# A two-layer routed transformer block: load semaphores, branch order and who compares, changed in three places

## The chip, the cores and the metric

The kernel runs on one core of one Trainium2 chip. The metric is the device time of one execution in microseconds (us); the time given for a kernel is the median over its runs. TensorE, VectorE, ScalarE, GpSimd and SyncE (which here only issues DMAs) are named PE, DVE, ACT, POOL and SP in the rows of the profile, PEld is the weight-load side of TensorE.

## The reference, cut to what matters

The input is x of 16 sequences by 256 tokens by 256. Layer 0 is causal attention (16 heads of 64, one key/value head, an added bias, a null key, and a mask of the keys), a layer norm, and then a top-1 router with a capacity; layer 1 is two further mixture layers, which the change does not touch.

```python
logits = tokens @ router_w.T                      # 4096 tokens, 8 experts
top1_idx = jnp.argmax(probs, axis=-1)
top1_prob = jnp.max(probs, axis=-1)
order = jnp.lexsort((-top1_prob, top1_idx))       # by expert, then by falling probability
...
keep_sorted = pos_in_group < capacity             # 640 places for each expert
return jnp.where(keep, top1_idx, 0)               # who finds no place goes to expert 0
```

So each token needs its place among the tokens of its expert: how many have a larger probability, or the same and a smaller number.

## The kernel before, in words

**Two cases.** The mask marks keys that may be seen, and in the data given only the last 64 positions of each sequence have any. The first DVE instructions reduce the mask to one number (`early_i`); every engine reads it (`early_keys`, L578) and branches. In the late case, the one that runs, attention, routing and the first experts are computed only for the last 64 positions of the 16 sequences, 1024 tokens, and one null row that stands for all others. In the general case all 4096 tokens are computed; that code is in the program but is not run.

**How TensorE's code lies.** Each engine's program is a straight list with branches. TensorE's (from L1322) has `If(late)` with attention and ranking (`late_rank`), then the `Else` with the whole general case, then a second `If(late)` with `late_table` and the experts. After ranking, TensorE therefore branches over the general code.

**The start.** SP issues the mask, two chunks of x (`x_l`), then g_in and wkv on the semaphore `ld_q` (L655, L656), reads `early_i`, and issues wq on the same semaphore (L659). Whoever waits for g_in or wkv waits for `ld_q` at 48, that is for wq too: TensorE before the key/value projection (`project_late_kv`, L1117 and L1121), ACT before it scales the turned rows by g_in (`late_rows`, L1691), DVE before it copies the key weights (L2164). The query projection `project_late_q` (L1128) needs wq. Then come the scores (`late_scores`, L1136), DVE's biased scores (L2103, L2106, L2107), ACT's exponential (L1712), DVE's probabilities (L2112 to L2115), the transposes (`turn_late`, L1143), the weighted sum (`weigh_late`, L1150) and the output projection (`project_late_o`, L1156).

**Attention's loop.** There are 8 chunks of 128 rows, `attend_late(c)` on each engine. On TensorE, chunk c computes scores, projects keys and queries of chunk c+1, waits for `v_ev` at c+2 (values of c+1, written by DVE's `late_values`, L2084), projects the output of chunk c-1, waits for the probabilities and turns them. DVE computes, in chunk 0 only, statistics of the other six chunks of x (`rest_stats`, L2143 and L2147) before `late_values(1)`. GpSimd adds the mask to the bias (`masked_bias`, L892), which DVE's L2103 waits for.

**The ranking.** The 1024 keys (probabilities) lie one per partition in `key_l`, 8 columns, and once more as one row repeated in all partitions: PE turns them into banks 0 and 1, ACT copies them to `rows_s` in SBUF (L1788, on `l_rows_ev`). For each column m of 128 tokens the matrix `beats[m]` (128 by 1024, bf16) holds whether key m is larger than the row's (for tokens up to this block, "is_lt", width (m+1)·128, L2417 on DVE or L907 on GpSimd) or not smaller ("is_le" for the later blocks, width (7-m)·128, L2423; for m = 0 in two pieces, L2419 and L2421), and `tied[m]` (L2424) settles equal keys inside the block. DVE does all of it but the "is_lt" of m = 5, 6, 7, which GpSimd does (`NGB = 3`). TensorE sums `beats[m]` against the one-hot choices, 9 small matmuls for each m (L1248, L1249), in the order m = 0 to 7:

```python
for m in range(NTW):
    pe.wait_ge(l_beat, m + 1)
    if m >= NTW - NGB:
        pe.wait_ge(l_beat_g, m - NTW + NGB + 1)
```

DVE takes the sums up at L2434 and goes through some 50 small dependent instructions; TensorE builds the row table (`late_table`, L1258), DVE writes it (L2487, semaphore `table`), GpSimd gathers the first expert's rows (`gathers`, L910; it waits for `table` just before its branch), TensorE turns them (L1273) and multiplies by the first weights (`expert_up`, L1285).

**Memory and loads.** The weights w1 (8 MB) are loaded from 16.8 us on (L712), w2 (8 MB) from 121.8 us on (L723).

## Time and profile before

| | |
|---|---|
| median of 3 runs | 596.69 us (596.47 to 598.17) |
| the profiled execution's own time | 598.48 us |
| its span, first to last instruction | 596.7 us |
| mean granted TensorE clock | 0.968 |
| TensorE busy | 539.6 us (90%) |
| VectorE busy | 319.9 us (54%) |
| ScalarE busy | 237.2 us (40%) |
| GpSimd busy | 235.7 us (39%) |

The page gives the busy time of each engine and the chain of waits that ended last, followed back from the last instruction. A busy share is a mean over stages; which engine sets the pace is read from a stage's timeline, where each group has its start, its duration, and in brackets how long its engine had been idle and what ended that.

### The profile page before, as it was taken

The numbers are of one execution on the slowest core, as the hardware profiler recorded it, in microseconds if no ns is written. First come the engines' busy times: TensorE is split into PE (matmuls) and PEld (weight loads), VectorE is DVE, ScalarE is ACT, GpSimd is POOL, SyncE is SP. The second block draws the span as 40 slices with busy tenths as digits, with TensorE's granted clock in tenths as the row PEclk, the third lists the DMA queues.
The fourth block names the chain that finished last, engine by engine and source line by source line (L and its number), as shares of the span: only waits on it lengthen the run. The fifth ranks groups of instructions, "written<-read, shape, count | busy, mean of one in ns | idle before, by whom it ended". The sixth has DMA issues, their size and how long they took to land.

```text
span 596.7 us, 11286 instructions
## 1 busy us (share of the span) xinstructions
PE 539.6 (90%) x3716; PEld 458.0 (77%) x3716; DVE 319.9 (54%) x968; ACT 237.2 (40%) x663; POOL 235.7 (39%) x319
## 2 busy tenths in 40 slices
PE   2899998941899999999999999999999998998885
PEld 2788886721799999998878978888888786776664
DVE  2767758577122224752537954444444354666564
ACT  1465445520111111115544245555555454443432
POOL 1412211041211121004825465555555078777860
PEclk9999999875799999999999999999999999999998
DMA  6980000185996531522378025665555324655552
GB/s 127 345 345 2 1 2 1 63 361 215 279 311 229 181 113 47 152 89 63 89 238 268 1 64 154 161 161 160 158 158 150 93 72 124 186 172 173 168 168 74
DMA packets 53205, 88.28 MB, mean 148 GB/s; under 512 B 11250, under 2 KB 43891, under 8 KB 51604
## 3 DMA queue, kind: packets, MB, share of 16 engines
q1 hardware_dynamic: 45028, 65.29, 31.7%
q0 software_dynamic: 8112, 22.16, 15.4%
q8 instruction: 36, 0.59, 0.4%
q14 instruction: 29, 0.24, 0.1%
HBM read 62.38 MB, written 25.04 MB: 146 GB/s over the span
## 4 chain that ended last, share of the span: by engine, by line
PE 71%; POOL 13%; issue 6%; DVE 5%; DMA 3%; ACT 2%; SPq 1%; DVEq 0%; POOLq 0%; ACTq 0%
POOL arena L910 11%; PE psum L1285 10%; PE psum L1524 10%; PE psum L1296 9%; PE psum L1443 7%; PE psum L1156 6%; PE psum L1538 5%; PE psum L1128 5%; PE psum L1453 3%; PE psum L1516 3%; POOL iota_i L939 2%; PE psum L1136 2%; PE psum L1471 1%; PE psum L1532 1%; PE psum L1150 1%
## 5 line engine op out<-in xcount | busy, mean ns | idle before, releaser
L910 POOL DMA_INDIRECT arena<-x,row_tok x71 | 68.3, 962 | 53.5 <-PE psum L1516 44.4
L910 POOL DMA_INDIRECT arena<-y_sorted,pos_k_i x64 | 65.3, 1021 | 35.8 <-DMA y_sorted<-arena 15.6
L1524 PE MATMUL psum<-big_w,arena 128*128 x284 | 72.9, 379 | 0.0
L1820 ACT ACTIVATE arena<-psum,arena 128x128 f32<-128x128 f32 x64 | 18.3, 368 | 118.2 <-PE psum L1285 88.0
L1285 PEld LDWEIGHTS psum<-arena,big_w 128*128 128x128 f32 x512 | 61.6, 197 | 2.8 <-issue 1.2
L1285 PE MATMUL psum<-arena,big_w 128*128 128x128 f32 x512 | 62.0, 281 | 1.5 <-DVE arena L2506 1.5
L1590 PE MATMUL psum<-big_w,arena 128*128 x256 | 63.3, 380 | 0.0
L1443 PE MATMUL psum<-arena,big_w 128*128 128x256 f32 x256 | 59.9, 381 | 0.2 <-ACT arena L1839 0.2
L1524 PEld LDWEIGHTS psum<-big_w,arena 128*128 128x128 f32 x284 | 53.7, 190 | 7.2
L1296 PE MATMUL psum<-arena 128*128 128x256 f32 (+1 forms) x256 | 57.7, 379 | 0.0
L2742 DVE SCALAR_TENSOR_TENSOR arena<-arena 128x128 f32<-128x128 f32 x71 | 20.8, 293 | 60.8 <-ACT arena L1906 60.4
L1443 PEld LDWEIGHTS psum<-arena,big_w 128*128 128x128 f32 x256 | 47.2, 190 | 7.1 <-ACT arena L1839 0.9
L1296 PEld LDWEIGHTS psum<-arena 128*128 128x128 f32 x256 | 47.5, 190 | 5.8
L1590 PEld LDWEIGHTS psum<-big_w,arena 128*128 128x128 f32 x256 | 46.4, 189 | 6.3 <-issue 0.5
L910 POOL DMA_INDIRECT arena<-h_late,row_tok x16 | 15.4, 963 | 86.1 <-PE psum L1273 72.8
L1538 PE MATMUL psum<-big_w,arena 128*128 x142 | 44.1, 392 | 0.7 <-ACT arena L1903 0.7
L892 POOL TENSOR_TENSOR arena<-arena 128x512 f32<-128x512 f32 x16 | 19.1, 1195 | 57.7 <-DVE arena L2107 57.6
L1156 PE MATMUL psum<-arena 128*128 128x256 f32 x144 | 34.5, 395 | 2.4 <-ACT arena L1707 1.6
L1903 ACT COPY arena<-psum 128x256 f32<-128x256 f32 x71 | 26.5, 373 | 22.6 <-PE psum L1538 22.2
L1156 PEld LDWEIGHTS psum<-arena 128*128 128x128 f32 x144 | 27.8, 198 | 7.4 <-issue 2.4
L1128 PE MATMUL psum<-arena 128*128 128x128 f32 x256 | 31.9, 285 | 0.0
L1453 PE MATMUL psum<-big_w,arena 128*128 128x256 f32 x128 | 30.6, 382 | 1.3 <-ACT arena L1843 1.3
(322 smaller groups left out, 961.3 us busy)
## 6 DMA issues: line engine op xcount, KB each, us to landing
y_sorted<-arena SPq DMA_DIRECT2D x71, 128.0 KB
big_w<-w SPq DMA_DIRECT2D x8, 1024.0 KB, 4.7
tokens<-x SPq DMA_DIRECT2D x4, 1024.0 KB, 14.9
x<-tokens SPq DMA_DIRECT2D x16, 256.0 KB, 2.8
z_kept<-arena SPq DMA_DIRECT2D x16, 256.0 KB
out<-arena SPq DMA_DIRECT2D x16, 256.0 KB
y_late<-arena SPq DMA_DIRECT2D x16, 128.0 KB, 1.7
big_w<-expert_w_t SPq DMA_DIRECT2D x1, 2048.0 KB, 7.5
```

The costliest lines, as they stand in the source:

```text
L910: pool.indirect_dma_start(dst, None, rows, bass.IndirectOffsetOnAxis(ap=idx, axis=0)).then_inc(done, 16)
L1128: mm = pe.matmul(bank[a][:, (j % 4) * P:(j % 4 + 1) * P], wq_s[:, k, j * P:(j + 1) * P], xt_l[:, k, :], start=k == 0, stop=k == KD - 1)
L1156: mm = pe.matmul(bank[6][:, 0:D], lhs(j), wo_s[:, j, :], start=j == 0, stop=j == NPAIR - 1)
L1285: mm = pe.matmul(bank[1 + 2 * u + f // 4][:, (f % 4) * P:(f % 4 + 1) * P], big_w[:, c:c + P], g_t[:, k, :], start=k == 0, stop=k == KD - 1)
L1296: mm = pe.matmul(bank[5 + j % 2][:, 0:D], act_t[j % 2][:, f, :], arena[:, bass.ds(e * (NF * D) + f * D, D)], start=f == 0, stop=f == NF - 1)
L1443: mm = pe.matmul(bank[up_bank(b) + q][:, half * S:(half + 1) * S], w[:, k, q * M1:(q + 1) * M1], p_s[:, unit(b)[1][k], :], start=k == 0, s ...
L1453: mm = pe.matmul(bank[6][:, n * D:(n + 1) * D], mid[u][q][:, n * P:(n + 1) * P], md_s[:, E1 + q, :], start=q == 0, stop=q == NSH - 1)
L1524: mm = pe.matmul(bank[2 + i % RT][:, 0:2 * M1], c_gt[i % RT][:, k, :], mgu_s[:, k, bass.ds(e, 1), :].rearrange("p a m -> p (a m)"), start= ...
L1538: pe.matmul(bank[5][:, 0:D], c_midt[i % RT], md_s[:, bass.ds(e, 1), :].rearrange("p a d -> p (a d)"), start=True, stop=True).then_inc(c_dn, 1)
L1590: mm = pe.matmul(o, z_t[u][:, k, n * P:(n + 1) * P], ew_s[:, k, bass.ds(e, 1), :].rearrange("p a d -> p (a d)"), start=False, stop=n == NB ...
L1903: act.copy(c_y[t % RT], bank[5][:, 0:D]).then_inc(c_yc, 1)
L2742: dve.scalar_tensor_tensor(c_mid[v], c_leak[v], 0.01, c_leak[v], ALU.mult, ALU.max).then_inc(c_lkd, 1)
```

## The change

It has four parts. (1) g_in and wkv get a semaphore of their own (`ld_kv`, the same one as `ld_wo`), and key/value work waits for these two alone; wq keeps `ld_q`, waited for at 16. (2) DVE computes `late_values(1)` before `rest_stats` in chunk 0. (3) TensorE's general code comes first in the program, the late case last and in one piece, so that the branch over the general code is taken at the start; and GpSimd waits for `table` after its branch. (4) The comparisons are shared out anew: GpSimd takes the "is_le" of m = 1 and the "is_lt" of 5 and 3; ACT takes the "is_lt" of 7, 6 and 4, each as Relu(key - row) followed by Sign; TensorE sums in the order 0, 1, 2, 5, 7, 3, 6, 4.

```diff
-        NGB = 3
+        G_LT, A_LT, G_LE = (5, 3), (7, 6, 4), 1
+        over = [tokens[:, NC - 6 - 2 * u:NC - 4 - 2 * u, :].rearrange("p c d -> p (c d)").bitcast(BF16) for u in range(2)]
...
+        ld_kv = ld_wo
+        l_beat_a, l_beat_a0 = xsd, 2
+        l_over, l_over0 = x_ev, NTW
...
             for dst, src in ((gin[:, :], g_in), (wkv_r, wkv.rearrange("(k p) n -> p k n", p=P))):
-                sp.dma_start(dst, src).then_inc(ld_q, 16)
+                sp.dma_start(dst, src).then_inc(ld_kv, 16)
...
+                sp.wait_ge(ld_kv, 32)
                 sp.dma_start(wo_s, wo.rearrange("(j p) n -> p j n", p=P)).then_inc(ld_wo, 16)
...
                 pool.wait_ge(l_rows_ev, 2)
-                for m in range(NTW - NGB, NTW):
+                pool.tensor_scalar(beats[G_LE][:, (G_LE + 1) * P:], rows_s[:, (G_LE + 1) * P:], key_l[:, G_LE:G_LE + 1], None, ALU.is_le).then_inc(l_beat_g, 1)
+                for m in G_LT:
                     pool.tensor_scalar(beats[m][:, 0:(m + 1) * P], rows_s[:, 0:(m + 1) * P], key_l[:, m:m + 1], None, ALU.is_lt).then_inc(l_beat_g, 1)
...
-            pool.wait_ge(table, 1)
             with pool.If(general):
...
             with pool.Else():
                 pool.wait_ge(l_hs, 48)
+                pool.wait_ge(table, 1)
                 gathers(TILES_L, h_late, True)
...
-                    pe.wait_ge(ld_wo, 16)
+                    pe.wait_ge(ld_wo, 48)
...
-                for m in range(NTW):
+                order = (0, 1, 2, 5, 7, 3, 6, 4)
+                for n, m in enumerate(order):
                     pe.wait_ge(l_beat, m + 1)
-                    if m >= NTW - NGB:
-                        pe.wait_ge(l_beat_g, m - NTW + NGB + 1)
+                    if m == G_LE:
+                        pe.wait_ge(l_beat_g, 1)
+                    if m in G_LT:
+                        pe.wait_ge(l_beat_g, G_LT.index(m) + 2)
+                    if m in A_LT:
+                        pe.wait_ge(l_beat_a, l_beat_a0 + A_LT.index(m) + 1)
...
             pe.wait_ge(const, NCONST)
-            late = early_keys(pe) == 0
-            with pe.If(late):
+            general = branch(pe)
+            with pe.If(general):
+                pe.sem_inc(turned, NPN)
...
+                experts(TILES, False)
+            with pe.Else():
                 turn_late_x(0)
-                pe.wait_ge(ld_q, 48)
+                pe.wait_ge(ld_kv, 32)
                 pe.wait_ge(setup, 1)
                 project_late_kv(0)
+                pe.wait_ge(ld_q, 16)
                 project_late_q(0)
...
                 late_rank()
-            with pe.Else():
-                pe.sem_inc(turned, NPN)
...
-                experts(TILES, False)
-            with pe.If(late):
                 late_table()
                 experts(TILES_L, True)
...
-                act.wait_ge(ld_q, 48)
+                act.wait_ge(ld_kv, 32)
                 late_rows(0)
...
+                act.wait_ge(l_rows_ev, 2)
+                for n, m in enumerate(A_LT):
+                    w = (m + 1) * P
+                    if n >= 2:
+                        act.wait_ge(l_beat_a, l_beat_a0 + n - 1)
+                    act.activation(over[n % 2][:, 0:w], rows_s[:, 0:w], ACT.Relu, bias=key_l[:, m:m + 1], scale=-1.0).then_inc(l_over, 1)
+                    act.wait_ge(l_over, l_over0 + n + 1)
+                    act.activation(beats[m][:, 0:w], over[n % 2][:, 0:w], ACT.Sign).then_inc(l_beat_a, 1)
...
+                if not last:
+                    late_values(c + 1)
                 if c == 0:
                     rest_stats()
-                if not last:
-                    late_values(c + 1)
...
-                dve.wait_ge(ld_q, 48)
+                dve.wait_ge(ld_kv, 32)
...
-                    if m < NTW - NGB:
+                    if m not in G_LT and m not in A_LT:
                         dve.tensor_scalar(beats[m][:, 0:(m + 1) * P], rows[:, 0:(m + 1) * P], key, None, ALU.is_lt)
...
-                    elif m < NTW - 1:
+                    elif m < NTW - 1 and m != G_LE:
                         dve.tensor_scalar(beats[m][:, later], rows[:, later], key, None, ALU.is_le)
```

How the instructions stand, at the places where it matters (in these listings branches are shown, waits are not, and equal neighbours are one row).

VectorE in the ranking, before, from the comparisons of m = 1 on (TENSOR_SCALAR is a comparison, SCALAR_TENSOR_TENSOR the settling of equal keys):

```order
L2417 TENSOR_SCALAR arena<-psum,arena 128x256
L2423 TENSOR_SCALAR arena<-psum,arena 128x768
L2424 SCALAR_TENSOR_TENSOR arena<-psum,arena,before 128x128
L2417 TENSOR_SCALAR arena<-psum,arena 128x384
L2423 TENSOR_SCALAR arena<-psum,arena 128x640
L2424 SCALAR_TENSOR_TENSOR arena<-psum,arena,before 128x128
L2417 TENSOR_SCALAR arena<-psum,arena 128x512
L2423 TENSOR_SCALAR arena<-psum,arena 128x512
L2424 SCALAR_TENSOR_TENSOR arena<-psum,arena,before 128x128
L2417 TENSOR_SCALAR arena<-psum,arena 128x640
L2423 TENSOR_SCALAR arena<-psum,arena 128x384
```

And in the changed kernel, the same stretch:

```order
L2439 TENSOR_SCALAR arena<-psum,arena 128x256
L2446 SCALAR_TENSOR_TENSOR arena<-psum,arena,before 128x128
L2439 TENSOR_SCALAR arena<-psum,arena 128x384
L2445 TENSOR_SCALAR arena<-psum,arena 128x640
L2446 SCALAR_TENSOR_TENSOR arena<-psum,arena,before 128x128
L2445 TENSOR_SCALAR arena<-psum,arena 128x512
L2446 SCALAR_TENSOR_TENSOR arena<-psum,arena,before 128x128
L2445 TENSOR_SCALAR arena<-psum,arena 128x384
```

Three comparisons are gone: 768 wide (m = 1), 512 wide (m = 3) and 640 wide (m = 4).

TensorE at the row table, before: the end of the general case (L1296 is an expert's second product) and then the second `If(late)`, where the late case arrives by a branch from behind L1253:

```order
L1296 MATMUL psum<-arena 128x256
L1370 UNCONDITIONAL_BRANCH
L1405 COMPARE_AND_BRANCH
L1258 MATMUL psum<-arena 128x16 x8
L1273 MATMUL psum<-ident,arena 128x128 x2
L1285 MATMUL psum<-arena,big_w 128x128 x16
```

In the changed kernel the same instructions follow the ranking directly:

```order
L1261 MATMUL psum<-arena 128x8 x8
L1262 MATMUL psum<-arena 128x8
L1266 MATMUL psum<-arena,ones 128x8
L1271 MATMUL psum<-arena 128x16 x8
L1286 MATMUL psum<-ident,arena 128x128 x2
L1298 MATMUL psum<-arena,big_w 128x128 x16
```

ScalarE behind its copies of the keys' row (L1801), in the changed kernel; the six activations are new, and no table load stands between them:

```order
L1796 ACT_TABLE_LOAD
L1796 ACTIVATE act_warm<-eps_col 128x1
L1798 ACTIVATE arena<-arena 128x72
L1801 COPY tokens<-psum 128x512 x2
L1807 ACTIVATE tokens<-tokens,arena 128x1024
L1809 ACTIVATE arena<-tokens 128x1024
L1807 ACTIVATE tokens<-tokens,arena 128x896
L1809 ACTIVATE arena<-tokens 128x896
L1807 ACTIVATE tokens<-tokens,arena 128x640
L1809 ACTIVATE arena<-tokens 128x640
```

## Rows read from the trace of the kernel before

**Rows 1.** The page, section 4: chain of work that ended last, shares by engine.

```profile
PE 71%; POOL 13%; issue 6%; DVE 5%; DMA 3%; ACT 2%; SPq 1%; DVEq 0%; POOLq 0%; ACTq 0%
```

**Rows 2.** Timeline 0 to 20 us (start us, us, engine, line, op, xcount [idle <-releaser]).

```profile
7.07 0.69 PE L1111 MATMUL psum<-ident,arena 128*128 128x128 f32 x2 [7.07 <-DVE arena L2080]
...
10.54 0.63 ACT L1691 ACTIVATE arena<-psum,gin 128x128 f32<-128x128 f32 x2 [4.18 <-DMA arena<-wq]
...
13.04 5.29 PE L1128 MATMUL psum<-arena 128*128 128x128 f32 x32
...
16.21 0.37 DVE L2170 COPY arena<-nb_bc 64x8 f32<-64x8 f32 x2 [5.16 <-DMA nb_bc<-null_bias]
...
17.73 2.36 POOL L892 TENSOR_TENSOR arena<-arena 128x512 f32<-128x512 f32 x2
...
19.78 0.70 DVE L2103 TENSOR_TENSOR arena<-psum,arena 128x520 f32<-128x520 f32 x1 [1.75 <-PE psum L1136]
```

**Rows 3.** DMA issues, 0 to 60 us (KB each, median us from issue to landing).

```profile
arena<-wo SPq DMA_DIRECT2D x1, 1024.0 KB, 7.2
...
arena<-wkv SPq DMA_DIRECT2D x1, 128.0 KB, 2.5
```

**Rows 4.** Timeline, end of chunk 0, 23 to 31 us.

```profile
23.94 2.05 DVE L2143 BATCH_NORM_STATS2 arena<-arena 128x6 f32<-128x256 f32 x6
...
26.70 3.72 PE L1156 MATMUL psum<-arena 128*128 128x256 f32 x16 [0.86 <-DVE arena L2084]
...
29.09 0.69 DVE L2115 TENSOR_TENSOR arena<-arena 128x512 f32<-128x512 f32 x1
...
30.26 1.04 PE L1143 MATMUL psum<-ident,arena 128*128 128x128 f32 x8
```

**Rows 5.** Timeline, the comparisons, 127 to 137 us.

```profile
127.08 7.54 POOL L907 TENSOR_SCALAR arena<-tokens,arena 128x768 bf16<-128x768 f32 x3 [32.02 <-ACT tokens L1788]
...
135.59 0.60 DVE L2424 SCALAR_TENSOR_TENSOR arena<-psum,arena,before 128x128 bf16<-128x128 f32 x2
...
136.25 0.37 PE L1248 MATMUL psum<-arena 128*128 128x8 bf16 x8
...
136.75 0.22 DVE L2434 TENSOR_TENSOR arena<-psum,arena 128x64 f32<-128x64 f32 x1 [0.18 <-PE psum L1249]
```

**Rows 6.** Groups by line and shape, 125 to 137 us (busy us, mean ns).

```profile
L907 POOL TENSOR_SCALAR arena<-tokens,arena 128x768 bf16<-128x768 f32 x1 | 2.2, 2217 | 32.0 <-ACT tokens L1788 32.0
...
L2423 DVE TENSOR_SCALAR arena<-psum,arena 128x768 bf16<-128x768 f32 x1 | 1.0, 1009 | 0.0
...
L2423 DVE TENSOR_SCALAR arena<-psum,arena 128x512 bf16<-128x512 f32 x1 | 0.7, 743 | 0.0
```

**Rows 7.** Groups by line and shape, ScalarE, 0 to 160 us.

```profile
L1774 ACT CAST arena<-iota_f 128x1024 f16<-128x1024 f32 x1 | 1.1, 1083 | 0.0
```

**Rows 8.** Chain of waits, 143 to 147 us (start us, us, what).

```profile
144.37 0.99 issue
```

**Rows 9.** Timeline, row table to first expert, 146 to 158.5 us.

```profile
146.07 0.17 DVE L2487 CAST row_tok<-psum 128x16 int32<-128x16 f32 x1 [0.37 <-PE psum L1258]
...
147.31 1.19 POOL L910 DMA_INDIRECT arena<-h_late,row_tok  x1 [12.70 <-issue]
...
151.82 5.86 PE L1285 MATMUL psum<-arena,big_w 128*128 128x128 f32 x32 [0.79 <-DVE arena L2506]
...
157.51 0.38 PE L1273 MATMUL psum<-ident,arena 128*128 128x128 f32 x2
...
158.17 0.95 POOL L910 DMA_INDIRECT arena<-h_late,row_tok  x1 [5.92 <-PE psum L1273]
```

**Rows 10.** DMA queues, 138 to 139 and 142 to 143 us (packets, MB, share).

```profile
q8 instruction: 1, 0.02, 5.5%
...
q8 instruction: 1, 0.02, 5.8%
```

**Rows 11.** Timeline, last output projections, 104 to 111 us.

```profile
104.77 5.38 PE L1156 MATMUL psum<-arena 128*128 128x256 f32 x16 [1.59 <-ACT arena L1707]
```

More of the change, by code:

```diff
@@ L931, in _ @@
                 pool.wait_ge(l_hs, 48)
+                pool.wait_ge(table, 1)
                 gathers(TILES_L, h_late, True)
@@ L1241, in late_rank @@
                 mm.then_inc(l_out, 1)
-                for m in range(NTW):
+                order = (0, 1, 2, 5, 7, 3, 6, 4)
+                for n, m in enumerate(order):
                     pe.wait_ge(l_beat, m + 1)
-                    if m >= NTW - NGB:
-                        pe.wait_ge(l_beat_g, m - NTW + NGB + 1)
+                    if m == G_LE:
[4 more added lines that the diff above has]
+                        pe.wait_ge(l_beat_a, l_beat_a0 + A_LT.index(m) + 1)
                     for c in range(NTW):
-                        pe.matmul(bank[4][:, c * E0:(c + 1) * E0], beats[m][:, c * P:(c + 1) * P], oh_l[:, m, :], start=m + c == 0, stop=False)
-                    mm = pe.matmul(bank[4][:, m * E0:(m + 1) * E0], tied[m], oh_l[:, m, :], start=False, stop=m == NTW - 1)
+                        pe.matmul(bank[4][:, c * E0:(c + 1) * E0], beats[m][:, c * P:(c + 1) * P], oh_l[:, m, :], start=n + c == 0, stop=False)
+                    mm = pe.matmul(bank[4][:, m * E0:(m + 1) * E0], tied[m], oh_l[:, m, :], start=False, stop=n == NTW - 1)
                 mm.then_inc(l_won, 1)
```

64 lines of the change are left out of this document (33 added, 31 removed).

## The prediction

> **What bounds the kernel now.** I read the page's chain first: 71% of the span is TensorE's, 13% GpSimd's [rows 1]. It names the engines, not the places, so I went on to the timeline of the stages that the change touches, all before 160 us. There TensorE is not the pace. At the start it waits for the first rows (7.07 us), then ACT, which scales them, waits till 10.54 for the load of wq, which it does not use, and the query projection starts at 13.04 [rows 2]. In chunk 0 the output projection waits until 26.70 for a small DVE instruction (L2084) that stands behind the statistics, which begin at 23.94 [rows 4]. In the ranking DVE is the pace and TensorE follows it [rows 5]. Behind it come two gaps: 0.99 us with no work at all before the row table [rows 8], and 1.07 us from the table's end (146.07 + 0.17) to GpSimd's gather at 147.31 [rows 9]. From chunk 1 on TensorE runs without gaps, so a shift at the end of chunk 0 is handed down to all that follows.
>
> **The sum, part by part.** Less than 1.8 us (0.3%) is about what a measurement can't tell from no change.
>
> Start. wkv lands 2.5 us after its issue, before 7 us [rows 3], so ACT may begin when the transposes end, 7.07 + 0.69 = 7.76, not at 10.54: 2.8 us earlier. Scaling and the key/value projection together lie between 10.54 and 13.04, 2.5 us, and would end near 10.3; the query projection then waits for wq, which landed at 10.5, and starts at 10.55 instead of 13.04, a gain of 2.5. Not all of it counts. DVE's first biased scores (L2103, at 19.78) also need the masked bias, which GpSimd starts at 17.73, two instructions in 2.36, so the first is ready at 17.73 + 1.18 = 18.91; its inputs hang on the load that ends at 16.21 [rows 2], which does not move. What is late next is thus the mask, and the gain there is 19.78 - 18.95 = **0.83**. The changed wait for wo costs nothing: wo lands 7.2 us after its issue at 16.3, at 23.5 to 24 [rows 3], and is needed at 25 or later.
>
> Chunk 0. DVE's L2084 goes ahead of the statistics, 2.05 us and their sums [rows 4]. The output projection loses its 0.86 of waiting beyond the shift of 0.83 and ends at 28.7 instead of 26.70 + 3.72 = 30.4. The transposes behind it (30.26) need DVE's last probabilities, which ended at 29.09 + 0.69 = 29.78 [rows 4] and move by 0.83 to 28.95: they start at 29.0. So DVE becomes the bound, and the two edits together give 30.26 - 29.0 = **1.25** (0.83 if the reorder gives nothing).
>
> Comparisons. DVE loses three: 768, 512 and 640 wide. The first two took 1.009 and 0.743 [rows 6], the third lies midway at 0.876; neighbours overlap by 0.08 each, so 2.63 - 0.25 = 2.38 us. DVE's last one ended at 135.59 + 0.60 = 136.19, now 133.81. TensorE had one group of nine matmuls left, 0.4 us (136.25 to 136.65) [rows 5]; now the groups of 7, 3, 6 and 4 are left, and behind each other each takes 0.26 more: 133.86 + 0.41 + 3 x 0.26 = 135.05. DVE goes on at 135.1 instead of 136.75: **1.6**. The cover must hold: GpSimd's three take at most 3 x 2.217 = 6.65 from 127.08 [rows 5, 6], 133.7, and its last is wanted at 134.3; ACT's six, at most 1.083 each (the 1024-wide cast [rows 7]), end by 133.5 plus the gaps between them (0 to 0.2 each), 134.5 at worst, and the last is wanted at 134.8. If that cover goes, TensorE waits for them one for one.
>
> Order of the cases. TensorE no longer branches between ranking and row table. The 0.99 us that nothing explains [rows 8] stand just behind that branch; in them no engine works, and instruction blocks came in at 138 and 142 us [rows 10]. I take the branch for the cause: **0.99**, bounds 0 and 0.99. GpSimd's branch goes ahead of its wait: 1.07 shrinks to the delay of a gather that waits for TensorE without a branch, 158.17 - (157.51 + 0.38) = 0.28 [rows 9]: **0.8**, bounds 0 and 0.8. In exchange TensorE takes the long branch at about 5 us. It costs nothing as long as the first transposes, at 7.07 now, start by about 9.0, for from there the way through both projections just meets the mask at 18.95; later than that, it costs one for one. The nearest price is the row table: from the branch at 138.1 at the latest to 145.36, at most 7.2 us; the bounds are 0 and 12.1 - 9.0 = 3.1. I take 0.
>
> The Trainium skill (Runtime: NRT & Kernel Launch, Instruction fetch mechanics) speaks against that exchange: a taken branch to code that is not at hand holds execution until a block is fetched. Here no row shows a branch of TensorE at 5 us; by that rule there is a fetch on both sides of the exchange, and it is one of the rivals below.
>
> Sum: 1.25 + 1.6 + 0.99 + 0.8 = **4.65 us**. The profiled execution took 598.48, 1.79 above the median. One row accounts for that: sixteen matmuls of the output projection took 5.38 at a granted clock of half, against 3.72 in chunk 0 [rows 4, 11], 1.66 more. So the profiled run would give 593.8 with that fall of the clock, and the median without it 596.69 - 4.65 = **592.0**. How the clock falls is not mine to shift, but the first expert's 32 matmuls run at half clock for their first 4.3 us (5.86 [rows 9]), and that stretch may come out 2 us cheaper or dearer by where the new times fall: plus or minus 1.7 for the range.
>
> **The rivals.**
> (a) The branch at the start is paid for: the first transposes come at up to 12.1, the start costs up to 3.1 instead of 0, and the time is 595.1. For it: the 7.2 us at the row table. Against: those lay in a stretch with 8 MB of w2 in flight, while at 5 us only wkv and 1 MB of wq are.
> (b) The 0.99 us are not the branch's (a wake-up of TensorE, or code that is late in any order): 593.0. For it: the second block came at 142, long after the branch.
> (c) ACT or GpSimd become the bound of the ranking: ACT's dependent pairs are new here. With gaps of 0.5 between them ACT ends 1.2 us behind what TensorE wants: 593.2.
> (d) Slower: TensorE's code up to 25 us lies ready now; after a branch at 5 us every further block must be brought in, and from 16.8 to 44 us 8 MB of w1 are in flight. If a block is as late as the gap between the two at 138 and 142 us [rows 10], 4.7 us, one such block eats the whole gain and two give 592.0 + 9.4 = 601.4. It decides from 6.5 us of lost fetch time (4.65 + 1.8). Against: TensorE had a block during 16 to 44 us before too, with no gap behind it.
>
> **How the numbers follow.** Forecast 0.56, (a) 0.18, (b) 0.12, (c) 0.09, (d) 0.05. All but (d) and the far end of (a) are faster; faster by over 0.3% means below 594.9. Faster: 0.56 + 0.12 + 0.09, and half of (a) that ends below 594.9, with 0.02 off for the clock: 0.84. Same: the rest of (a), and the clock's share, 0.12. Slower: 0.04. The range goes from 592.0 - 1.7 = 590.3 to (a) at 595.0.
>
> **What would show it.** Right: the first projection of keys at 8.5 and DVE's first biased scores at 18.9, waiting for GpSimd; the transposes of chunk 0 at 29.0; DVE through with the comparisons 7.1 us after its first (9.5 now) and TensorE's last sums within 1.3 us of that; less than 0.2 us between DVE's one-hots and the row table; about 0.3 us from table to gather. Wrong: a TensorE start after 9 us (a), a gap of 1 us still before the row table (b), TensorE waiting for ACT or GpSimd in the sums (c), gaps of TensorE that end with no releaser between 5 and 44 us (d). If chunk 1 starts no earlier than 30.2, my reading of the start is wrong.

## The result, and the profile after

The change is faster. Over 17 runs each the median went from 596.45 to 593.58 us; the ratio is **0.9939, 95% interval 0.9926 to 0.9952**, or 3.6 us (2.9 to 4.4); the two medians by themselves are 2.9 us apart. One of the change's 17 runs took 1924.93 us and, as the only slow one, is left out of the ratio. The forecast was 592.0, range 590.3 to 595.0. The profiled execution took 594.12 us (span 592.3) against 598.48 (span 596.7).

Lines have moved: L1111 is now L1119, L1128 is L1136, L1143 is L1151, L1156 is L1164, L2103 is L2125, L2434 is L2456, L2487 is L2509, L910 is L917, L1285 is L1298.

The page's chain of the changed kernel hardly differs from [rows 1]: TensorE 68% for 71, GpSimd 14% for 13, VectorE 6% for 5.

```profile
PE 68%; POOL 14%; DVE 6%; issue 6%; SPq 2%; DMA 2%; ACT 1%; DVEq 0%; POOLq 0%; ACTq 0%
```

The timeline of the start, 0 to 20 us (start, us, engine, line, operation, operands [idle before <- what ended it]), to be read beside [rows 2]:

```profile
8.54 0.69 PE L1119 MATMUL psum<-ident,arena 128*128 128x128 f32 x2 [8.54 <-issue]
9.32 0.63 ACT L1704 ACTIVATE arena<-psum,gin 128x128 f32<-128x128 f32 x2 [2.83 <-PE psum L1119]
...
11.83 5.55 PE L1136 MATMUL psum<-arena 128*128 128x128 f32 x32
...
16.72 0.37 DVE L2192 COPY arena<-nb_bc 64x8 f32<-64x8 f32 x2 [9.16 <-DMA nb_bc<-null_bias]
...
18.26 2.37 POOL L898 TENSOR_TENSOR arena<-arena 128x512 f32<-128x512 f32 x2 [0.70 <-DVE arena L2197]
...
19.58 0.70 DVE L2125 TENSOR_TENSOR arena<-psum,arena 128x520 f32<-128x520 f32 x1 [1.01 <-POOL arena L898]
```

ACT now waits for TensorE and not for wq, and the query projection begins 1.2 us earlier. But TensorE's first transposes are 1.5 us later and end a wait on nothing shown ("issue"). The first biased scores, now held by GpSimd's mask, gained 0.20 us, because the null bias and with it the mask are 0.5 later than before.

The end of chunk 0, to be read beside [rows 4]: the output projection comes 1.2 us earlier, the transposes behind it 0.62 (29.64 against 30.26).

```profile
25.48 3.66 PE L1164 MATMUL psum<-arena 128*128 128x256 f32 x16
...
28.89 0.69 DVE L2137 TENSOR_TENSOR arena<-arena 128x512 f32<-128x512 f32 x1
...
29.64 1.09 PE L1151 MATMUL psum<-ident,arena 128*128 128x128 f32 x8 [0.50 <-DVE arena L2137]
```

The comparisons, 124 to 137 us, beside [rows 5]:

```profile
126.57 1.15 ACT L1807 ACTIVATE tokens<-tokens,arena 128x1024 bf16<-128x1024 f32 x1
126.63 2.21 POOL L912 TENSOR_SCALAR arena<-tokens,arena 128x768 bf16<-128x768 f32 x1 [32.14 <-ACT tokens L1801]
...
128.83 3.75 POOL L914 TENSOR_SCALAR arena<-tokens,arena 128x768 bf16<-128x768 f32 x2
...
131.47 0.74 ACT L1809 ACTIVATE arena<-tokens 128x640 bf16<-128x640 bf16 x1
...
132.66 0.60 DVE L2446 SCALAR_TENSOR_TENSOR arena<-psum,arena,before 128x128 bf16<-128x128 f32 x2
...
134.27 0.17 PE L1262 MATMUL psum<-arena 128*128 128x8 bf16 x1
...
134.55 0.22 DVE L2456 TENSOR_TENSOR arena<-psum,arena 128x64 f32<-128x64 f32 x1 [0.91 <-PE psum L1262]
```

ScalarE is done at 132.21 and GpSimd at 132.58, both before VectorE's last tie ends at 133.26, and TensorE's last sum ends at 134.44 (134.27 + 0.17). Only once does TensorE wait for a helper, 0.62 us for GpSimd's m = 1 at 128.99; the next group waits for VectorE again, so this costs nothing. From the first comparison (126.12, before 126.67) to the take-up of the ranks it is 8.43 us, before 10.08.

From the one-hots to the experts, beside [rows 8, 9]:

```profile
141.46 0.68 DVE L2497 TENSOR_TENSOR arena<-arena 128x1024 f16<-128x1024 f16 x1
...
142.20 0.69 PE L1271 MATMUL psum<-arena 128*128 128x16 f16 x8 [5.76 <-DVE arena L2497]
...
143.14 0.35 DVE L2507 CAST pos_i<-arena 64x8 int32<-64x8 f32 x2
143.50 0.17 DVE L2509 CAST row_tok<-psum 128x16 int32<-128x16 f32 x1
...
144.56 1.19 POOL L917 DMA_INDIRECT arena<-h_late,row_tok  x1 [11.98 <-issue]
...
148.97 5.28 PE L1298 MATMUL psum<-arena,big_w 128*128 128x128 f32 x32 [0.79 <-DVE arena L2528]
...
155.16 3.84 PE L1298 MATMUL psum<-arena,big_w 128*128 128x128 f32 x32 [0.70 <-DVE arena L2528]
```

The gap ahead of TensorE's row table is gone: 142.20 starts 0.06 us behind the one-hots, before it was 1.01. But the row numbers, which GpSimd waits for, show no idle time before them any more: VectorE works through its small operations without a pause until 143.50. From the start of the one-hots to the row numbers it is 2.04 us, before 2.40. The first expert starts 2.85 us earlier than in [rows 9], the second 3.44 (155.16 against 158.60), because the 32 matmuls between them took 5.28 us, before 5.86. From there every stage up to 350 us is 3.44 us earlier. What comes on top later in the profiled pair (4.21 us at the last output) arises in layer 2, where nothing was changed.

### The profile page after: what moved, and what is told of

Read it like the earlier page. It is cut to its first block, busy times and chain, and to the rows that moved or that the text cites. A ratio compares the mean times of both kernels' runs of the same rounds, so it can differ in the third digit from the quotient of the medians.

```text
span 592.3 us, 11290 instructions
## 1 busy us (share of the span) xinstructions
PE 537.5 (91%) x3716; PEld 457.6 (77%) x3716; DVE 318.3 (54%) x965; ACT 242.6 (41%) x669; POOL 233.3 (39%) x319
## 4 chain that ended last, share of the span: by engine, by line
PE 68%; POOL 14%; DVE 6%; issue 6%; SPq 2%; DMA 2%; ACT 1%; DVEq 0%; POOLq 0%; ACTq 0%
POOL arena L917 11%; PE psum L1298 10%; PE psum L1537 10%; PE psum L1309 9%; PE psum L1456 7%; PE psum L1551 5%; PE psum L1164 5%; PE psum L1136 4%; PE psum L1466 3%; PE psum L1529 3%; POOL iota_i L947 3%; PE psum L1144 1%; PE psum L1484 1%; PE psum L1545 1%; PE psum L1158 1%
## 5 line engine op out<-in xcount | busy, mean ns | idle before, releaser
L917 POOL DMA_INDIRECT arena<-x,row_tok x71 | 68.2, 960 | 51.9 <-PE psum L1529 43.4
L917 POOL DMA_INDIRECT arena<-y_sorted,pos_k_i x64 | 65.7, 1027 | 36.4 <-POOL iota_i L947 18.9
L1298 PEld LDWEIGHTS psum<-arena,big_w 128*128 128x128 f32 x512 | 61.0, 196 | 2.8 <-issue 1.2
L1298 PE MATMUL psum<-arena,big_w 128*128 128x128 f32 x512 | 61.4, 279 | 1.5 <-DVE arena L2528 1.5
L917 POOL DMA_INDIRECT arena<-h_late,row_tok x16 | 15.4, 960 | 84.7 <-PE psum L1286 72.1
L1164 PE MATMUL psum<-arena 128*128 128x256 f32 x144 | 34.5, 394 | 1.6 <-ACT arena L1720 1.6
L1136 PE MATMUL psum<-arena 128*128 128x128 f32 x256 | 32.1, 286 | 0.8 <-DVE arena L2129 0.8
L1164 PEld LDWEIGHTS psum<-arena 128*128 128x128 f32 x144 | 27.8, 198 | 6.4 <-issue 2.4
L2781 DVE SCALAR_TENSOR_TENSOR arena<-arena,w_k 128x256 f32<-128x256 f32 x64 | 28.2, 482 | 6.9 <-issue 5.2
```

The lines of the kernel that those rows point to most:

```text
L917: pool.indirect_dma_start(dst, None, rows, bass.IndirectOffsetOnAxis(ap=idx, axis=0)).then_inc(done, 16)
L1136: mm = pe.matmul(bank[a][:, (j % 4) * P:(j % 4 + 1) * P], wq_s[:, k, j * P:(j + 1) * P], xt_l[:, k, :], start=k == 0, stop=k == KD - 1)
L1164: mm = pe.matmul(bank[6][:, 0:D], lhs(j), wo_s[:, j, :], start=j == 0, stop=j == NPAIR - 1)
L1298: mm = pe.matmul(bank[1 + 2 * u + f // 4][:, (f % 4) * P:(f % 4 + 1) * P], big_w[:, c:c + P], g_t[:, k, :], start=k == 0, stop=k == KD - 1)
L2781: m = dve.scalar_tensor_tensor(z_s[u][:, n, :], yk[u][:, 2 * n + k, :], w_k[:, k, bass.ds(b * NB + n, 1)], base, ALU.mult, ALU.add)
```

## The experiments

For the runs the four parts of the change are taken as three, named here K (the key/value semaphore and the swap of values and statistics in chunk 0), O (TensorE's general case first in its program, so that the late case runs from the ranking into the row table without a branch, and GpSimd's branch ahead of its wait) and S (the shared comparisons). With the kernel before and the change itself, six runs complete the eight combinations. Each ratio is to the kernel before as it ran in the same job. The two edits inside K, and the two inside O, were not timed apart.

**K alone**, edit against the kernel before:

```diff
-                sp.dma_start(dst, src).then_inc(ld_q, 16)
+                sp.dma_start(dst, src).then_inc(ld_kv, 16)
-                act.wait_ge(ld_q, 48)
+                act.wait_ge(ld_kv, 32)
-                if c == 0:
-                    rest_stats()
                 if not last:
                     late_values(c + 1)
+                if c == 0:
+                    rest_stats()
```

> The kernel before with only the load semaphore of its own and the earlier values of chunk 1 (parts 1 and 2). Theory (the mask is what DVE's first biased scores wait for, and the block fetches of TensorE's branch at 5 us had held up the loads that the mask hangs on by 0.5 us): without that branch the first transposes are back at 7.1, the copy of the null bias on DVE at 16.2, the first biased scores at 18.95 and chunk 0's transposes at 29.0, 1.25 earlier than before; time 1.2 us below before. Rival (the 0.5 us are chance, nothing to do with the fetches): the copy of the null bias lies anywhere between 16.2 and 16.8, as in kernels with the branch. Rival (the start is worth only what the change showed, 0.6, because of the queue itself): first biased scores at 19.6 here too.

Measured 0.9991 (0.9974 to 1.0007). The forecast was 1.2 us, this is 0.5, and it can't be told from no change. In its profile the start gained more than the forecast gave it: mask 17.28, first biased scores 18.60 (before 19.78), turn of chunk 0 at 28.66 (before 30.26). Of that 0.39 us can't be put down to the edit: SyncE's issue of the null value, behind which the null bias is issued, took 2.79 us in this execution and 3.18 both before and in K and S. The branch gap stayed, 1.18 us.

**O alone**:

```diff
-            late = early_keys(pe) == 0
-            with pe.If(late):
+            general = branch(pe)
+            with pe.If(general):
...
-            with pe.If(late):
                 late_table()
                 experts(TILES_L, True)
```

> The kernel before with only part 3 (TensorE's rare case first in the program, GpSimd waiting for the table after its branch). Theory (the branch behind the ranking held TensorE 1 us, but DVE's own five small instructions ahead of the table take the place of that wait): the gap between DVE's one-hots and TensorE's row table falls from 0.99 to under 0.1, the table comes 0.35 us earlier, counted from the one-hots, and the gather 0.2 nearer to the table; time 0.5 us below before, less than its noise. TensorE's first transposes at 8.5 instead of 7.1, the null bias copied at 16.7; that costs nothing, since the key work waits for wq anyway. Rival (the gap belongs to TensorE's wake-up): the gap stays at 1 us. It did not in the change, so this rival would need parts 1 or 4 for it.

Measured 1.0026 (1.0009 to 1.0043): by itself this part costs 1.5 us, where 0.5 us of gain were expected. The start of its timeline:

```profile
8.05 0.69 PE L1112 MATMUL psum<-ident,arena 128*128 128x128 f32 x2 [8.05 <-DVE arena L2080]
10.68 0.62 ACT L1691 ACTIVATE arena<-psum,gin 128x128 f32<-128x128 f32 x2 [4.27 <-DMA arena<-wq]
...
11.45 1.19 PE L1118 MATMUL psum<-arena 128*128 128x128 f32 x4 [2.71 <-ACT arena L1691]
...
13.18 6.12 PE L1129 MATMUL psum<-arena 128*128 128x128 f32 x32
...
20.75 0.70 DVE L2103 TENSOR_TENSOR arena<-psum,arena 128x520 f32<-128x520 f32 x1 [2.34 <-PE psum L1137]
```

The query projection takes 6.12 us, before 5.29 [rows 2], because the clock rose at 18.0 and not at 16.2; the first biased scores are 1.0 us late. The gap at the row table is 0.07, but it returns only part of that. The profiled execution took 595.54 us, 2.0 less than this kernel's median, so its rows show where time can go and not that the 1.5 us went there.

**S alone**:

```diff
-        NGB = 3
+        G_LT, A_LT, G_LE = (5, 3), (7, 6, 4), 1
...
-                    if m < NTW - NGB:
+                    if m not in G_LT and m not in A_LT:
+                    act.activation(over[n % 2][:, 0:w], rows_s[:, 0:w], ACT.Relu, bias=key_l[:, m:m + 1], scale=-1.0).then_inc(l_over, 1)
```

> The kernel before with only part 4 (comparisons shared with ScalarE and GpSimd). Theory (DVE alone set the pace of the ranking): from DVE's first comparison to its take-up of the sums 10.08 us before, 8.4 here as in the change; time 1.65 us below before, and the 0.99 us ahead of the row table are back, as the branch is. Rival (the branch needs a fixed time from its block fetch on, hidden before by the ranking): as the ranking ends earlier, TensorE is not ready earlier, the gap grows from 1.0 to up to 2.6, and the part gives nothing by itself.

Measured 0.9973 (0.9955 to 0.9992). First comparison to take-up 8.43 us, before 10.08. The gap at the row table was expected back at 0.99 us, or by the rival grown to 2.6. With the branch still there it was 0.23 us, before 1.01, so both missed:

```profile
139.84 0.68 DVE L2492 TENSOR_TENSOR arena<-arena 128x1024 f16<-128x1024 f16 x1
...
140.75 0.67 PE L1267 MATMUL psum<-arena 128*128 128x16 f16 x8 [5.93 <-DVE arena L2492]
```

**K and S (the change without O)**: the diff of O taken back from the changed kernel.

```diff
-            general = branch(pe)
-            with pe.If(general):
+            late = early_keys(pe) == 0
+            with pe.If(late):
```

> The changed kernel with part 3 taken back. Theory (parts add, each by its stage): first transposes at 7.1, null bias copied at 16.2, first biased scores at 18.95, chunk 0's transposes at 29.0, gap ahead of the row table at least 1.0 again; time within 0.3 us of the changed kernel, since the start's 0.6 comes back and the row table's and the gather's 0.5 go. Rival (fixed time from the block fetch on, as in the run with part 4 alone): the gap is 2.6, time 1 to 1.5 us above the changed kernel.

Measured 0.9948 (0.9929 to 0.9966), gap 0.26 us instead of 1.0, and one-hots to row numbers 2.04 us: the same as in the change. O can't be told from nothing here. The first biased scores came at 19.07, near the forecast; chunk 0's transposes came at 30.74 instead of 29.0, as the clock fell to the low level from 19.4 to 26.2 us.

**O and S (the change without K)**:

```diff
-                act.wait_ge(ld_kv, 32)
+                act.wait_ge(ld_q, 48)
```

> The kernel before with TensorE's rare case placed last and with the shared comparisons, but without the key/value semaphore and without the swap of chunk 0's statistics and values. The start branch alone cost 0.26% in the kernel before, the shared comparisons alone gave 0.27%, the key/value part alone 0.09%. If the parts add: ratio 0.9999. If the three help each other (the whole gave 0.61% where the singles sum to 0.10%): the key/value part covers what the start branch costs, and this run lies near 0.997, with the first biased scores after 20.3 and the turn of chunk 0 after 30.8. Ratio of 0.994 would mean that the key/value part is worth nothing.

Measured 0.9976 (0.9958 to 0.9994), with the first biased scores at 20.28 and the turn of chunk 0 at 30.76.

**K and O (the change without S)**:

```diff
-        G_LT, A_LT, G_LE = (5, 3), (7, 6, 4), 1
+        NGB = 3
```

> The kernel before with the key/value semaphore, the swap of chunk 0 and TensorE's rare case placed last, but with the comparisons split as before (three of GpSimd, none of ScalarE). It completes the table of the three parts. Theory (parts: key/value -0.24%, order +0.07%, shared comparisons -0.40%, of which 1.6 us are the comparisons and 0.7 us the wait at the row table, which the branch's late code made): here the order part removes the wait at the table (0.06 instead of 1.0 to 1.2 us, of which VectorE's small operations keep about 0.65) and the start is covered, so the ratio is about 0.9985, with the first comparison to take-up 10.1 us. Rival (the order part is worth its 1.8 us when the key/value part covers its cost at the start): 0.996. Second rival (it costs as it did alone, 0.26%): 1.0015 or more.

Measured 0.9979 (0.9965 to 0.9992), first comparison to take-up 10.09 us, gap 0.07.

The eight ratios together:

| | neither K nor S | K | S | K and S |
|---|---|---|---|---|
| without O | 1 | 0.9991 | 0.9973 | 0.9948 |
| with O | 1.0026 | 0.9979 | 0.9976 | 0.9939 |

Each part's worth is the mean of its four differences: K -0.0030 (1.8 us), S -0.0040 (2.4 us), O +0.0002 (0.1 us slower). With intervals of some 0.0017 on each ratio, such a mean is good to about 0.7 us. So K and S are each shown to gain, and O is not shown to do anything on the whole.

**The branch gap.** Four of these kernels branch between ranking and row table. The trace has each DMA packet with its time; TensorE's own instruction queue fetched a second 16 KB block there. How its end stands to the row table, in us:

| kernel | second block ends | one-hots end | row table starts | block to table |
|---|---|---|---|---|
| before | 143.75 | 144.35 | 145.36 | 1.61 |
| K | 140.73 | 141.15 | 142.33 | 1.60 |
| S | 139.15 | 140.52 | 140.75 | 1.60 |
| K and S | 140.17 | 141.52 | 141.78 | 1.61 |

That made a forecast possible. The test puts matmuls that nothing reads between the kept counts and the branch of the kernel without O:

```diff
                 pe.matmul(bank[6][:, 0:E0], ones[:, :], ksum, start=True, stop=True).then_inc(l_out, 1)
+                for _ in range(12):
+                    pe.matmul(bank[7][:, 0:P], ident[:, :], ident[:, :], start=True, stop=True)
```

> The changed kernel with TensorE's two halves as before (the branch between the ranking and the row table is back) and 12 filling matmuls of float32 between the kept counts and that branch. In the four kernels that have the branch, TensorE's row table started 1.60 to 1.62 us after the end of the second 16 KB code block that TensorE fetches there. Theory (the wait of 1.0 us at the row table is that code coming late, and its request follows TensorE's own progress): with the filling ahead of the branch the second block is requested later, at 141 or after, the row table again starts 1.6 us after its end, and the wait behind the one-hots grows from 0.26 us to 1.5 us or more. Rival (the code is fetched ahead, whatever TensorE's queue does, and the wait is a plain cost of the branch): the wait stays between 0.2 and 1.2 us, and the distance of 1.6 us from the block breaks.

```profile
139.13 0.68 DVE L2503 TENSOR_TENSOR arena<-arena 128x1024 f16<-128x1024 f16 x1
...
142.80 0.68 PE L1275 MATMUL psum<-arena 128*128 128x16 f16 x8 [3.37 <-issue]
143.52 0.17 DVE L2515 CAST row_tok<-psum 128x16 int32<-128x16 f32 x1 [2.36 <-PE psum L1275]
...
144.76 1.19 POOL L917 DMA_INDIRECT arena<-h_late,row_tok  x1 [14.48 <-issue]
```

The filling ended at 139.4, the second block came from 140.25 to 141.20, and the table started 1.60 us after it. The gap grew to 2.99 us. The block began 8.03 us after the take-up of the ranks, in K and S 5.30 us after it. So the wait is code arriving late, and work in TensorE's queue ahead of the branch puts the code off. The Trainium skill (Runtime: NRT & Kernel Launch, Instruction fetch mechanics) says that a taken branch out of the code at hand forces a fetch before execution goes on; the trace agrees, with 1.60 us from the end of the fetch as a further part of the price. What exactly sets the request stays open: the block began 0.8 us after TensorE's last matmul here, and 3.4 to 4.3 us after it in the four kernels of the table. This kernel ran once (597.54 us), so its time says nothing.

The same run also tests the forecast for the start, as it has K and S and TensorE doesn't branch at 5 us in it. The null bias was copied at 16.09, the first biased scores came at 18.95 and chunk 0's transposes at 29.00; the forecast was 18.95 and 29.0, with the null bias at 16.2.

**Null transfers first**, against the change:

```diff
-                sp.dma_start(v_null, null_kv[1:2, :].rearrange("a d -> (a d)").partition_broadcast(P)).then_inc(ld_bias, 16)
                 load_null()
+                sp.dma_start(v_null, null_kv[1:2, :].rearrange("a d -> (a d)").partition_broadcast(P)).then_inc(ld_mask, 16)
-                pool.wait_ge(ld_bias, 80)
+                pool.wait_ge(ld_bias, 64)
-                dve.wait_ge(ld_bias, 80)
+                dve.wait_ge(ld_bias, 64)
+                dve.wait_ge(ld_mask, 32)
```

> The changed kernel, but SyncE issues the null bias and null column transfers ahead of the null value, and the null value counts on a semaphore of its own, so that GpSimd's causal fill waits for the four side transfers alone. Theory (the masked bias of GpSimd bounds the first biased scores, and its input is late): the null bias copy moves from 16.7 to about 14, GpSimd's fill from 14.99 to about 13.5, its mask from 18.26 to about 16.5 at most, the first biased scores from 19.58 to 18.8 (there TensorE's first scores are next), the turn of chunk 0's probabilities from 29.64 to about 28.9, and the kernel is 0.7 us faster than the changed one: ratio to the kernel before about 0.9927. Rival (key/value and query work of TensorE, at the low clock, bound the start): first biased scores stay at 19.4 or later and the ratio stays at 0.994. A second rival: the start gains but the end does not, because a later clock fall takes it: turn at 28.9, ratio 0.994.

```profile
9.20 4.05 SPq L672 DMA_DIRECT2D null_col<-null_kv  x2
13.30 0.59 SPq L672 DMA_DIRECT2D nb_bc<-null_bias  x1
...
16.09 0.37 DVE L2192 COPY arena<-nb_bc 64x8 f32<-64x8 f32 x2 [8.50 <-DMA nb_bc<-null_bias]
...
19.03 0.70 DVE L2125 TENSOR_TENSOR arena<-psum,arena 128x520 f32<-128x520 f32 x1 [1.02 <-POOL arena L898]
...
25.86 3.69 PE L1164 MATMUL psum<-arena 128*128 128x256 f32 x16 [0.77 <-issue]
```

And of its DMA issues (KB, us from issue to landing):

```profile
arena<-wo SPq DMA_DIRECT2D x1, 1024.0 KB, 8.9
```

GpSimd's fill came at 13.19 as expected, but the null bias was issued only 0.43 us earlier (13.30, in the change 13.73): SyncE's long issue, 3.01 us for the null value there, now befell the first of the two null columns (3.40 of the row's 4.05). The scores gained 0.55 and still wait for the mask, so the mask is the bound there. The turn gained 0.25, not 0.7: TensorE was free at 25.09, but the output projection started at 25.86. The load of wo, which it needs, was issued at 16.86 and landed at 25.8. So wo was the next bound, which no run tested by an edit. In the change it was close: issued at 16.82, landed 8.5 us later at about 25.4, and wanted at 25.48. The whole, 0.9933 (0.9908 to 0.9958), is too wide to show 0.3 us.

**Row numbers first**, against the change:

```diff
+                dve.wait_ge(tab_ps, 1)
+                dve.tensor_copy(row_tok[:, 0:TILES_L], bank[3][:, 0:TILES_L]).then_inc(l_in, 1)
                 bx = [P, TILES_L, E0 - 1]
...
-                pool.wait_ge(table, 1)
+                pool.wait_ge(l_in, 4)
```

> The changed kernel, but VectorE writes the row numbers right after the one-hots, ahead of the tile numbers and the null positions, on a semaphore that only GpSimd's gather waits for. Theory (in the changed kernel VectorE's seven small operations took the place of the wait for TensorE's row table, so that only 0.4 of the 1.0 us came through): row numbers 1.5 us after the start of the last one-hots instead of 2.04, gather and expert 0 about 0.55 us earlier, ratio to the kernel before about 0.993. Rival (the gap itself, or GpSimd's own wake-up, bounds the hand-over): the row numbers come earlier but the gather does not, its distance grows from 1.06 to 1.6 us, ratio 0.994.

```profile
141.35 0.69 DVE L2497 TENSOR_TENSOR arena<-arena 128x1024 f16<-128x1024 f16 x1
...
142.82 0.17 DVE L2499 CAST row_tok<-psum 128x16 int32<-128x16 f32 x1 [0.78 <-PE psum L1271]
143.87 1.19 POOL L917 DMA_INDIRECT arena<-h_late,row_tok  x1 [11.07 <-issue]
```

The row numbers come 1.47 us after the start of the one-hots, 0.57 sooner than in the change, and the gather keeps its distance (1.05). So VectorE's small operations had taken the place of the gap. The time, 0.9934 (0.9909 to 0.9959), can't show it by itself.

**Filling at two places**, against the change: the same matmuls, 12 behind the kept counts, 10 behind the row table.

```diff
+                idle_work(12)
...
                 mm.then_inc(tab_ps, 1)
+                idle_work(10)
```

> The changed kernel with 12 float32 matmuls 128 x 128 into an unused bank behind the kept counts and 10 more behind the row table, where TensorE idles 5.8 and 4.6 us; they write nothing that is read. At the low clock they take about 0.43 us each, 5.1 and 4.3 us, so they end before TensorE is wanted. Theory (the granted clock costs time at expert 0: it comes back only at 152.0, 3 us after the first expert's matmuls begin): the clock is high at 148, the 32 matmuls of expert 0 take about 3.5 us instead of 5.3, and the second expert starts 1.5 us earlier against the first; ratio to the kernel before 0.991. Rival (something else, ScalarE and VectorE or the gathers, paces the experts): matmuls faster, the second expert no earlier, ratio 0.994. If the filling matmuls delay the table or the rows: 0.995 or more.

The clock rose at 140.5 as hoped. The second filling then took 2.5 us at the high clock, TensorE idled 2.33, and at 147.3 the clock fell again: expert 0's matmuls took 5.44 us. So this kernel did not make the state that the theory is about, and tells nothing of its worth: 5.44 lies within the 5.20 to 6.09 us of the kernels without filling. Ratio 0.9931 (0.9904 to 0.9958).

**Null first, row numbers first and that filling:**

```diff
+                dve.tensor_copy(row_tok[:, 0:TILES_L], bank[3][:, 0:TILES_L]).then_inc(l_in, 1)
...
+                idle_work(12)
...
+                idle_work(10)
```

> The changed kernel with the null transfers first, the row numbers first and the smaller filling (12 and 10 matmuls at the two idle stretches around the row table). Singly they gave 0.55 us at the first biased scores, 0.57 us at the row numbers, and a clock that rose at 140.5 but fell again at 147.3, for 0.2 to 0.4 us at expert 0. If the gains add and reach the end: 1.5 us faster than the changed kernel, ratio 0.9915. If a gain at the start is lost again to the clock's own phase: 0.993.

Measured 0.9927 (0.9907 to 0.9947), which is not to be told from the change, nor from the 0.9915 that was hoped for. In this one the clock fell at 140.7, so the second filling took 4.03 us at the low clock and left no gap behind it; the clock was high from 144.1, the 32 matmuls took 3.81 us, and in the profiles the experts ran 7.64 us earlier than in the kernel before. The filling is that of the run above; what differed was when the clock changed. In layer 2 that lead shrank to 5.9 us; a fall of the clock at 560.5, for 3.4 us, is part of it.

**The same with filling in every idle stretch** from the logits to the first rows:

```diff
+                idle_work(8)
...
+                    idle_work((5, 1, 3, 6, 1, 0, 0, 0)[n])
...
+                idle_work(18)
...
+                idle_work(18)
```

> The changed kernel with the null transfers first, the row numbers written first, and float32 matmuls of 128 x 128 into an unused bank in every idle stretch of TensorE from the logits to the first rows (8, 5, 1, 3, 6, 1, 18 and 18 of them, sized to the high clock, 0.21 us each). Theory (the clock is held up if TensorE is never idle for long, and costs time at expert 0 otherwise): the granted clock stays high from 120 to the end, expert 0's 32 matmuls take about 3.7 us, the transposes ahead of the ranking and the rows are 0.2 to 0.3 us shorter each, and the kernel is 3 us faster than the changed one: ratio to the kernel before 0.989. Rival (the clock falls all the same, and the filling, at 0.43 us each, then delays the ranks by 2 and the table by up to 2.6 us): 0.996 or more. In between, the clock up in part: 0.992.

Measured **0.9902 (0.9873 to 0.9932)**, median 591.48 against 598.02 in the same job: faster than the kernel before. Against the change it is 0.0037, or 2.2 us, but the two intervals overlap a little, so that this kernel is faster than the change is likely and not shown. The profile shows where time went in one execution. Between 120 and 584 us the clock was low only from 133.5 to 136.9. Two windows of 6 us of each kernel (us; busy us of PE, PEld, DVE, ACT, POOL with counts; granted clock; DMA). First the change, then the two fillings, then the full one:

```profile
138.00:144.00 6.00, 0.69 (x8) 0.59 (x8) 5.29 (x29) 0.00 (x0) 0.00 (x0) 0.50 0.46 198
144.00:150.00 6.00, 1.69 (x7) 1.35 (x8) 2.18 (x11) 0.00 (x0) 3.08 (x3) 0.50 0.22 66
```

```profile
138.00:144.00 6.00, 5.24 (x39) 4.76 (x38) 5.35 (x32) 0.00 (x0) 0.97 (x1) 0.79 0.43 179
144.00:150.00 6.00, 3.20 (x15) 3.02 (x16) 0.79 (x3) 0.00 (x0) 2.11 (x3) 0.78 0.57 180
```

```profile
138.00:144.00 6.00, 5.67 (x54) 5.49 (x53) 4.67 (x27) 0.00 (x0) 1.88 (x2) 1.00 0.16 57
144.00:150.00 6.00, 5.14 (x44) 4.67 (x42) 0.88 (x4) 0.00 (x0) 1.21 (x2) 1.00 0.69 224
```

And its first two experts:

```profile
146.11 3.81 PE L1306 MATMUL psum<-arena,big_w 128*128 128x128 f32 x32 [0.79 <-DVE arena L2538]
...
150.84 1.38 PE L1306 MATMUL psum<-arena,big_w 128*128 128x128 f32 x10 [0.70 <-DVE arena L2538]
```

The 32 matmuls take 3.81 instead of 5.28, and the second expert follows the first after 4.73 us, in the change after 6.19. In the two profiles the experts are 4.3 us ahead of the change's, about: 1.46 by this, 0.57 by the row numbers, some 0.4 by the start, and 1.7 because the fall of the clock at 104 us [rows 11] did not happen in this execution, which the filling, all behind it, has no part in. The kernel with the smaller filling had come just as far: 3.81 us for the 32 matmuls, and the second expert at 150.88.

```profile
146.15 3.81 PE L1304 MATMUL psum<-arena,big_w 128*128 128x128 f32 x32 [0.79 <-DVE arena L2536]
```

So the profiles show no worth of the larger filling over the smaller one. That it makes the high clock at expert 0 more frequent is a guess.

## Why the prediction was right, and where it was not

The time was in the range, it went the way that was forecast, and the largest term held by its mechanism. 4.65 us were forecast and 3.6 measured by the ratio, 2.9 by the medians. Three of the terms came out smaller than forecast and the clock gave something back, so that the total is nearer than its parts. By its own terms:

1. **Comparisons, 1.6.** The profiles give 1.65 (10.08 to 8.43; 8.43 in all kernels with S but the fully filled one, 8.36), and the step's own working fits: VectorE's last end 133.26 less the first comparison 126.12 is 7.14, forecast 7.1; four groups are left, and TensorE's sums end at 134.44, 8.32 after the first comparison, forecast 8.38. ACT and GpSimd end ahead of need, so rival (c) fell. By the table S is worth 2.4, good to 0.7. Where the branch is there, a shorter ranking also shortens the gap behind it (1.0 to 0.23, so the row numbers follow the one-hots after 2.04 us instead of 2.40). But S gains no less beside O (0.0050 and 0.0040 against 0.0027 and 0.0043), where there is no gap, so this doesn't account for the difference, which stays open.
2. **Start, 0.83, with chunk 0 1.25.** Half right. That the mask would be next holds: the changed kernel's row names GpSimd's mask, and the first scores start 1.32 us behind the mask's start there, in K, in K and S, and in the run with filling ahead of the branch. In that last one both numbers of the forecast were met, 18.95 and 29.00; K alone gained 1.18 at the scores and 1.60 at the turn, 0.39 of it by a short issue of SyncE. In the change it was 0.20 and 0.62. The swap in chunk 0 did its part: the output projection waits 0.85 to 0.86 us for VectorE in the four kernels without K and not at all for it in those with K. The step that failed is the sentence "its inputs hang on the load that ends at 16.21, which does not move". It moved by 0.51, to 16.72. SyncE's four issues of the side took exactly 2.60 us in before, K, S and K with S, where TensorE doesn't branch at 5 us (2.68 in the one with filling ahead of the branch), and 2.79 to 3.64 in all nine kernels where it does and fetches a block at 5.5 to 5.7. The threshold of 9.0 for the first transposes was not passed (8.54), so it was not TensorE's own lateness, rival (a) as I put it, but SyncE's. That the fetch lengthens SyncE's issues is argued from this split, and no experiment moved it alone. Nor is the wait for wo free for good: the sum had it land at 23.5 to 24, and in the change it landed at about 25.4, just ahead of 25.48.
3. **The branch gap, 0.99.** The cause was right: the gap goes with the branch (0.07 us or less in all nine kernels without it), so rival (b) fell, and it is code that comes late, as the run with filling ahead of the branch showed. The worth was wrong. The term took the whole gap without asking what is late next: VectorE's small operations, 1.36 us from the end of the one-hots to the row numbers, stood in the trace of before too, hidden by the gap. So 0.36 of 0.99 came through. Beside S even that is no gain of O, since K and S without O has the same 2.04.
4. **GpSimd's branch, 0.8.** Wrong size. From the start of the row numbers to the gather it is 1.24 to 1.26 us in the kernels with the branch behind the wait and 1.05 to 1.06 in those with it ahead: 0.19. The row that I priced it by is of a later gather; the first one takes longer for another reason, which stays open.
5. **The clock, plus or minus 1.7**, was needed. The high clock came back in expert 0 at 152.0, before at 156.1, which gave 0.58 of the 3.44 us; that is luck of the time at which it rose. It shows in the total too: of the change's 16 fast runs the five with a mean granted clock of 0.975 took 590.5 to 591.6 us, the eleven with 0.970 to 0.974 took 592.5 to 595.4. The fall at 104 us was in both profiles (5.38 us for the output projection in each), but in only two of the twelve others.

Sum as measured at the second expert: 0.55 at the first comparison + 1.65 + 0.36 + 0.18 + 0.58 = 3.3, the rest of the 3.44 are roundings and hand-overs of 0.1. Forecast for the same place was 4.65 without the clock. Rival (d), blocks late after the start, did not show: TensorE fetched nine blocks between 20 and 105 us, before eight, and from the turn of chunk 0 to the first comparison it took 96.5 us, before 96.4.

## What to carry to other kernels

When an edit removes a wait, look at who else waits for the same event: the engine that worked under its cover is the next bound, and its end is in the old trace. An edit that put a taken branch earlier moved a code fetch rather than removing it; put the branch where the engine has slack, and count the neighbours' DMA issues too. Where an engine idles for a few us ahead of dense matmul work, compare the duration of the first matmuls with later ones of the same shape: 5.28 against 3.81 us is 1.47, more than the row numbers first gave (0.57) and nearly as much as the shared comparisons (1.65).

## What the runs showed of the hardware

- After a taken branch TensorE's work began 1.60 or 1.61 us after the last packet of its 16 KB block, five times out of five at the row table, and the first transposes began 1.49 to 1.57 us after it in the nine kernels that branch at the start; the block itself took 0.9 to 1.5 us.
- The granted clock rose at 12.3 to 18.0 us in profiles whose first transposes differed by less than 1.6 us. In the four where it rose between 15.5 and 16.5 it fell at 104 to 105 us for 3.4 us, and in the ten others it did not. In two, where it rose at 12.5 and 12.8 (K and S, and row numbers first), it was low again from about 19.5 to 26.3 us with TensorE busy (5.57 and 5.34 us of the 6 from 18 to 24). In K and S the query projection of chunk 1 took 6.16 us instead of 3.84, and the turn of chunk 0 came at 30.74 instead of 29.64 although the first scores had been earlier. In K alone the clock rose at 12.3 and did not fall there, so the time of the rise does not settle it. This is why single profiles of these kernels differ by 2 us and stages must be compared one by one.
- One issue of SyncE at about 9 us took 2.79 to 3.44 us in all fourteen kernels, its neighbours about 0.6, whichever transfer stood there (the null value in the change; the first null column when these go first, 3.19 to 3.40). Moving the null value past it moved the stall to the null column.
